# A routed expert phase: no weight copies ahead of the rows, six dense blocks first and two last, fourteen constant matmuls before the phase

## What is computed

```
x = x + xattn(layernorm(x), ctx)                     # 1024 rows of 128, context of 6404 rows
s = layernorm(x)
expert_id = argmax(s @ wr + br)                      # one of 8 experts for each row
h = gelu(s @ w1[e] + b1[e])                          # 128 -> 512, exact gelu
y = h @ w2[e] + b2[e]                                # 512 -> 128
out = x + y of the row's own expert
```

## Time and profile before

| | |
|---|---|
| median of three runs | 232.77 us |
| the profiled execution, whole | 234.39 us |
| its span | 232.7 us |
| PE busy in the span | 201.1 us, 86% |
| DVE busy | 180.6 us, 78% |
| ACT busy | 157.9 us, 68% |
| POOL busy | 128.6 us, 55% |
| mean granted clock of TensorE | 0.944 of full |

### The profile page before, as it was taken

One profiled execution on the slowest core, in us unless ns is written; L12 is line 12 of the kernel. 1 busy time (PEld: TensorE's weight loads), 2 busy tenths in 40 slices (PEclk: granted clock), 3 DMA queues, 4 the chain that ended last, 5 costly groups with the idle time before them and its releaser, 6 DMA issues.

```text
span 232.7 us, 5011 instructions
## 1 busy us (share of the span) xinstructions
PE 201.1 (86%) x1837; PEld 150.3 (65%) x1837; DVE 180.6 (78%) x395; ACT 157.9 (68%) x249; POOL 128.6 (55%) x177
## 2 busy tenths in 40 slices
PE   0379969999999999989989899899993797999980
PEld 0133417776766767757666566789973686899970
DVE  2899797697998998998995997958756435776872
ACT  2752899399399699699595799689531445667650
POOL 3695718807915807978508947744400740066763
PEclk9999985899999999999999999999996569999998
DMA  6999979899999999999999999988994369999200
GB/s 215 389 251 263 226 223 237 192 234 174 220 215 216 278 230 269 241 198 233 216 213 256 184 220 258 201 196 185 239 263 121 120 219 290 346 370 378 98 11 12
DMA packets 142958, 51.78 MB, mean 223 GB/s; under 512 B 121172, under 2 KB 140773, under 8 KB 142934
## 3 DMA queue, kind: packets, MB, share of 16 engines
q1 hardware_dynamic: 142000, 50.08, 93.2%
q0 software_dynamic: 784, 1.38, 1.7%
q10 hardware_dynamic: 150, 0.00, 0.0%
HBM read 10.74 MB, written 3.75 MB: 62 GB/s over the span
## 4 chain that ended last, share of the span: by engine, by line
PE 49%; DVE 21%; DMA 11%; issue 8%; ACT 4%; POOL 3%; SPq 2%; DVEq 0%; POOLq 0%
DMA PT<-Phl 10%; PE psX L1079 5%; PE psS L1061 5%; PE psO L1079 5%; PE psS L1060 5%; PE psS L1059 5%; DVE S L800 5%; DVE Phl L817 3%; PE psS L1290 3%; PE psX L1081 3%; PE psO L1081 3%; ACT S L651 3%; SPq L393 2%; PE psS L1276 2%; PE psS L1296 2%
## 5 line engine op out<-in xcount | busy, mean ns | idle before, releaser
L651 ACT ACTIVATE S<-S,negb 128x1024 f32<-128x1024 f32 x48 | 55.1, 1147 | 18.4 <-DVE negb L808 18.4
L800 DVE TENSOR_SCALAR_CACHE_REDUCE S<-psS 128x1024 f32<-128x1024 f32 x48 | 58.2, 1217 | 11.4 <-PE psS L1061 11.2
L817 DVE TENSOR_TENSOR Phl<-S,Phl 128x1024 f16<-128x1024 f32 x38 | 51.5, 1355 | 5.0 <-ACT Phl L666 4.8
L533 POOL TENSOR_TENSOR Phl<-S,Phl 128x256 f16<-128x256 f32 x40 | 26.3, 689 | 51.7 <-ACT Phl L666 51.7
L666 ACT CAST Phl<-S 128x1024 f16<-128x1024 f32 x48 | 50.3, 1047 | 5.2 <-DMA PT<-Phl 3.7
L1059 PE MATMUL psS<-qT,gh 128*128 128x512 f16 x96 | 37.7, 393 | 5.4 <-DVE S L800 2.6
L1079 PE MATMUL psX<-qn,PT 128*128 128x256 f16 x204 | 36.4, 273 | 2.1 <-DMA PT<-Phl 2.1
L1079 PE MATMUL psO<-qn,PT 128*128 128x256 f16 x204 | 37.3, 276 | 0.9 <-DMA PT<-Phl 0.8
L1061 PE MATMUL psS<-qT,gl 128*128 128x512 f16 x96 | 37.9, 395 | 0.0
L1060 PE MATMUL psS<-qT,gh 128*128 128x512 f16 x96 | 37.9, 394 | 0.0
L1081 PE MATMUL psO<-qn,PT 128*128 128x128 f16 x204 | 35.7, 221 | 0.0
(11 more groups left out here) (239 smaller groups left out, 425.3 us busy)
## 6 DMA issues: line engine op xcount, KB each, us to landing
PT<-wp SPq DMA_DIRECT2D x8, 512.0 KB, 6.0
stageT<-in_ctxT SPq DMA_DIRECT2D x6, 512.0 KB, 7.0
qn<-wp SPq DMA_DIRECT2D x6, 512.0 KB, 7.3
wp<-in_w SPq DMA_DIRECT2D x4, 512.0 KB, 4.9
stageT<-in_w SPq DMA_DIRECT2D x4, 512.0 KB, 4.9
rows_by_expert<-stageT SPq DMA_DIRECT2D x4, 385.5 KB, 5.6
PT<-Phl SPq DMA_TRANSPOSE x48, 4.2
S<-rows_by_expert SPq DMA_DIRECT2D x2, 258.0 KB, 5.4
```

The source lines that it names most:

```text
L533: last = nc.gpsimd.tensor_tensor(lo[:, r], slot(t, e)[:, r], hi[:, r], ALU.subtract)
L651: nc.scalar.activation(slot(t, e), slot(t, e), ACT.Exp, bias=negb[:, t:t + 1], accum_out=Lp[:, t * NG + e:t * NG + e + 1]).then_inc(exp_do ...
L800: nc.vector.tensor_scalar(out=into, in0=bank(u, n)[:, 0:into.shape[1]], scalar1=1.0 / GS, scalar2=None, op0=ALU.mult, op1=ALU.max, accum_o ...
L817: nc.vector.tensor_tensor(lo, slot(t, e), hi, ALU.subtract).then_inc(low_done, 1)
```

## The change

Three things are changed. `DENSE_AT` puts six dense blocks first and two last (before: five first, and one each at 10, 16 and 21). SyncE loads all fourteen expert numbers at once, and the copies of weights for sent blocks 0 and 1 move from ahead of the wait for the scatters to behind it, one behind the first and one behind the second batch of rows. TensorE gets fourteen matmuls whose result nobody reads: two ahead of the ranks and twelve behind the counts, each 128 by 128 weights and 512 columns of a constant.

```diff
-    DENSE_AT = (0, 1, 2, 3, 4, 10, 16, 21)
+    DENSE_AT = (0, 1, 2, 3, 4, 5, 20, 21)
-    FIRST = 2
...
             sp.wait_ge(experts_ready, 1)
-            sp.reg_load(expert_reg[0:FIRST], bexp[0:1, 0:FIRST])
-            ex = [sp.snap(r, min_val=0, max_val=E - 1) for r in expert_reg[0:FIRST]]
+            sp.reg_load(expert_reg[0:NB], bexp[0:1, 0:NB])
+            ex = [sp.snap(r, min_val=0, max_val=E - 1) for r in expert_reg]
...
-            for b in range(FIRST):
-                fetch(b)
-            sp.reg_load(expert_reg[FIRST:NB], bexp[0:1, FIRST:NB])
-            ex += [sp.snap(r, min_val=0, max_val=E - 1) for r in expert_reg[FIRST:NB]]
             sp.wait_ge(rows_sent, 16 * TA)
             block_rows(0, 0, D, rows_landed)
+            fetch(0)
             block_rows(1, 0, D, rows_landed)
+            fetch(1)
             fetch(2)
...
+            filler = ones[:, :].bitcast(F16)
+            def fill(n):
+                for _ in range(n):
+                    nc.tensor.matmul(psS[2][:, 0:CH], filler[:, 0:P],
+                                     filler.unsqueeze(1).broadcast_to([P, 2, 2 * P]), start=True, stop=True)
+            fill(2)
             pe.wait_ge(chosen_ready, 1)
...
             last.then_inc(ranks_in_psum, 1)
+            fill(12)
             pe.wait_ge(x2n_ready, H + 1)
```

## The result

The changed kernel takes **238.08 us** (median of four runs, 236.64 to 239.93) against 232.91 for the kernel before, measured beside it: **1.0188 times, 95% interval 1.0141 to 1.0235, slower**. The forecast was 232.5 with a range of 231.0 to 234.4. A later measurement gave 237.51 against 234.43, 1.0047 times (1.0004 to 1.0091): slower in both, by how much is less sure.

A forecast was written before the change was run, and what follows sets the result against it. TensorE was taken to be on the path, with the DMA of routed rows close behind. 0.0 at batch 2, -0.4 and +0.1 at the end gave -0.3: 234.1 us profiled, 232.5 median, range 231.0 to 234.4.

The forecast's parts named there:

- Six dense blocks at full clock end at 191.2: Dense blocks before the first routed rows: from 182.4 all six end 2.4 us earlier than the five of before.
- The copies come back later: SyncE's queue before batch 2: two copies add 2.8 us, less 1.9 for a moved instruction load; rows land at 204.6.
- a load of instructions falls again among the rows: Slower rival, between the first rows' issue and batch 2: batch 2 starts at 206.5, +1.9, 234.4 us; chance 0.12.
- the clock's fall behind the wait: Slower rival at the wait ahead of batch 2: next block runs at 1.2 GHz, +1.5, 234.0 us; chance 0.12.
- Without the early copies the rows leave 0.4 earlier: Row scatters and first-batch issue: with the two early weight copies gone, rows leave 0.4 us earlier (bounds 0 and -0.4).
- Two fills ahead of the ranks, +0.1: TensorE between its fp32 work and the ranks: two fills delay the path by 0.1 us (bounds 0 and +0.3).
- a delay over 0.3: Sign of a wrong forecast: the scatters start more than 0.3 us later than before.
- is the same in both kernels: Attention half, ahead of the changed code: taken as unchanged, since only the last quarter of the program differs; no time priced.
- The end: Last two blocks dense, results in one plain copy, GpSimd's last scatter off the path: -0.4 us (bounds -0.3 and -0.8).
- faster dense blocks only gain a wait for the rows: Between dense blocks and batch 0: the clock's whole gain of 2.4 us turns into a wait of 2.2 us.

The follow-up runs named there:

- e7: The changed kernel with its seven indirect row scatters replaced by plain stores of the same rows: 233.24 us against 234.43 for the kernel before (0.9900 to 0.9974).
- e10: The changed kernel with each of the seven row scatters waiting until the data of the one before have landed: 246.48 us, one run.
- e4: The kernel before with only the two weight copies moved behind the first rows and all expert numbers loaded at once: 236.72 us against 234.85.
- e13: The kernel before with fourteen small constant matmuls behind TensorE's last instruction: 1.0021 times the kernel before (0.9987 to 1.0055).
- the repeat: The changed kernel measured again, unaltered, on the same chip as later variants: 237.51 us against 234.43 for the kernel before (1.0004 to 1.0091).

## Why the prediction was wrong

- **"Six dense blocks at full clock end at 191.2": the step that failed first.** The price of a block came from a stretch without back-to-back scatters; the dense blocks lie beside seven of them. The blocks took 14.2 us instead of 8.8 (183.82 to 198.06), because TensorE's signals were held until the last scatter and the clock then fell (193). e7 and e10 show the cause, the row scatters issued back to back. The trace of before had the sign of it: the gelu of block 2 at 190.49 began 1.8 us behind the end of its `up`; it cost nothing there, since the first rows landed only when the slow blocks ended.

```profile
190.49 0.60 ACT L710 ACTIVATE Phl<-psS 128x512 f16<-128x512 f32 x1 [2.34 <-remote]
```

- **"The copies come back later": the size was right, the deduction from it wrong.** Two copies cost 2.5 us up to batch 2 (e4, 30.8 against 28.3 in the kernels without a wait there, before and e13 at 28.1 to 28.5), near the 2.8 forecast. I took 1.9 off because the load of instructions would leave that stretch; it came again at 207.3. And 1.9 was too much to take off: in the trace of before the last sixteenth of the batch-1 rows landed 1.8 us behind the others (196.46 and 194.66), but that of the batch-2 rows only 0.9 (204.03 and 203.17). The rival "a load of instructions falls again among the rows", given 0.12, is what happened, and the clock's fall behind the wait, also 0.12, with it. That fall is not fixed: in the repeat the wait was longer (2.99 us) and its clock stayed at 1.00 through the slice at 210.
- **"Without the early copies the rows leave 0.4 earlier": wrong cause.** The scatters are 0.96 each in the change, but the 1.33 of before has nothing to do with the copies (e4). The first batch was issued 2.4 later: the scatters start 1.6 later, 0.4 comes off, and 1.2 more lie between the last scatter and the issue, where the load of instructions stands.
- **"Two fills ahead of the ranks, +0.1": right in size.** Ranks start 0.65 us behind the attention; before 0.62. The fills sit in the wait that was there. The scatters start 1.6 us later because the attention ends later; the prediction had named a delay over 0.3 as a sign of being wrong.
- **The attention half "is the same in both kernels" (the section on the kernel before): wrong, and in the main unexplained.** In all ten profiles with fills in the middle the attention ends at 175.9 to 178.6 us, mean 177.3; in the ten without at 174.2 to 176.1, mean 175.3. TensorE's list is the same up to there. These 2.0 us are part of the loss of every kernel with fills. The traces show where they arise. TensorE's first matmul starts at 8.4 to 8.8 us with fills in the middle and at 8.7 in e13, against 7.6 to 8.3 in the other nine: half a microsecond seems to go with the longer program, and e13 still has it at 101 us. Most of the next 1.0 comes at one wait of the attention for a transposed copy, near 102 us: on average 1.5 us with fills, 0.8 without, 0.5 in e13. The change and the kernel before there:

```profile
103.78 0.28 PE L1076 MATMUL psX<-qn,PT 128*128 128x256 f16 x1 [2.14 <-DMA PT<-Phl]
...
102.03 0.28 PE L1079 MATMUL psX<-qn,PT 128*128 128x256 f16 x1 [0.76 <-DMA PT<-Phl]
```

Why this copy is later in the kernels with fills stays open.
- **The end: right in direction, outside its bounds in size.** From the last issue to the end it is 1.3 us shorter; -0.4 was forecast, with bounds of -0.3 and -0.8.

Together, from the profiles: 2.0 us in the attention half, 1.8 from the stoppage under the fills and 2.6 from the copies, 6.4 taken singly; the two profiles of the change lie 5.5 and 4.4 above the one of before, its medians 5.2 and 3.1, so the parts overlap. The forecast had seen that faster dense blocks only gain a wait for the rows; it had not seen that they would not be fast.

## What to carry to other kernels

An engine's price from one stretch holds in another only if the neighbours are alike: look at what GpSimd and the DMAs do beside it, and compare the end of a matmul group with the start of its reader, not with the next matmul. Lifting TensorE's clock ahead of a phase whose data come late gains nothing by itself; what leads to the data (scatters, issue, copies in the same queue) has to be shortened first. And work taken out of a waiting time and put behind the wait is paid in full when the transfers behind it are the next bound.

## What the runs showed of the hardware

Seven indirect scatters of rows, issued 0.30 us apart by GpSimd, hold up TensorE's completion signals: the gelu of block 2 started 4.62 us behind the last row of its `up` in the change and 4.72 in the repeat. One signal of ScalarE in that time was not late (its gelu ended at 186.45, VectorE's next row started at 186.48); VectorE worked until 188.05 and then stood 3.97 us. Scatters of results at the same distance did not hold the signals at 225.88 (0.04 us). By the Trainium skill, "Perfetto Trace Analysis", section "DMA Instruction — SWDGE (GPSIMD)", the row of such a scatter ends when its descriptors are written, not when its data have moved; the trace agrees (last row ends at 190.67, first batch released at 193.49). Which of the two holds TensorE is not settled: in e10 both the data and the descriptors had gaps. While a load of 16 KB of instructions was under way or just done (191.31 to 192.27 and 207.27 to 208.37 in the change), one sixteenth of a transfer landed behind the others, by 1.3 us in the last row scatter and by 1.6 us in batch 2, and the whole transfer counted as landed only then; in the repeat it was 1.9 and 1.4 us. That the load makes it late is read from these times; no run moved a load alone.
